# The tail of a five-part layer: products over two scan tiles at once, residual sums on TensorE, token moves spread over eight rounds

## The reference, cut to what matters

```
# branch 1: two Mamba scans, forward and over the flipped sequence (256 inner channels, 16 states)
h = exp(dt_t[..., None] * A) * h + (dt_t * u_t)[..., None] * B_t[:, None, :]
y_t = einsum('bdn,bn->bd', h, C_t)
...
y = (y + u * D) * silu(z);  out = einsum('bld,ed->ble', y, Wout)
# branch 2: attention over 16 heads, then one of 8 experts for each token
x = x + (o @ wo + bo)
hn2 = layernorm(x) * ln2_g + ln2_b
idx = argmax(hn2 @ gate_w + gate_b, axis=-1)
mid = relu(einsum('th,ehf->etf', hn2, w1) + b1[:, None, :])
y = einsum('etf,efh->eth', mid, w2) + b2[:, None, :]
moe = y[idx, arange(T)];  out = x + moe
# the layer
x = x + branch1(xn) + branch2(xn)
```

## Time and profile before

| | us |
|---|---|
| runs | 1390.32, 1390.54, 1390.70 |
| median | 1390.54 |
| profiled execution, its own time | 1392.7 |
| its span, first to last instruction | 1391.0 |
| begin of the tail stage | 874.5 |
| first scan tile to end of the last | 877.1 to 1379.0 |

### The profile page before, as it was taken

One profiled execution on the slowest core, in us unless ns is written; L12 is line 12 of the kernel. 1 busy time (PEld: TensorE's weight loads), 2 busy tenths in 40 slices (PEclk: granted clock), 3 DMA queues, 4 the chain that ended last, 5 costly groups with the idle time before them and its releaser, 6 DMA issues. The chain is left out here.

```text
span 1391.0 us, 18267 instructions
## 1 busy us (share of the span) xinstructions
PE 969.8 (70%) x5897; PEld 314.5 (23%) x5897; DVE 1212.5 (87%) x1837; ACT 871.9 (63%) x1298; POOL 520.8 (37%) x484
## 2 busy tenths in 40 slices
PE   3789986888888888888888888434326775743243
PEld 1443321111111111111111111212103443411011
DVE  8872668999999999999999980799989997978997
ACT  6445557777777777777777789444346665644332
POOL 4030116000000000000000000669899997979985
PEclk9999997999999999999999999655557988865555
DMA  3033333100000320000011000144578778785540
GB/s 96 0 139 132 125 125 141 49 1 1 1 28 27 62 58 13 20 28 17 16 32 28 6 14 2 44 89 108 133 183 181 179 182 203 182 204 122 122 103 8
DMA packets 88865, 111.49 MB, mean 80 GB/s; under 512 B 15603, under 2 KB 46122, under 8 KB 88770
## 3 DMA queue, kind: packets, MB, share of 16 engines
q1 hardware_dynamic: 87746, 108.22, 29.9%
q0 software_dynamic: 1024, 2.10, 0.6%
HBM read 84.43 MB, written 25.56 MB: 79 GB/s over the span
## 5 line engine op out<-in xcount | busy, mean ns | idle before, releaser
L829 DVE TENSOR_REDUCE at_mpart<-psum 128x1 f32<-128x512 f32 x1024 | 637.9, 684 | 44.4 <-PE psum L977 41.0
L805 ACT ACTIVATE at_probs<-psum 128x1024 f32<-128x1024 f32 x512 | 495.2, 1021 | 147.5 <-PE psum L1005 147.2
L1328 POOL TENSOR_TENSOR t_inject<-shared 128x512 f32<-128x512 f32 x256 | 326.1, 1304 | 31.3 <-DMA shared<-mp_dtu_d 18.6
L1018 PE MATMUL psum<-at_probs,at_vg 128*32 128x512 f32 x2048 | 274.8, 609 | 0.5 <-ACT at_probs L805 0.4
L977 PE MATMUL psum<-at_ks,at_qs 56*128 56x512 bf16 x1024 | 203.3, 394 | 100.4 <-DVE at_mpart L829 99.6
L1687 PE MATMUL psum<-t_hc,stack 128*32 128x512 f32 x512 | 108.1, 929 | 190.6 <-DVE t_hc L1502 180.9
L698 POOL CAST at_m<-at_mneg 128x16 bf16<-128x16 f32 x16 | 3.1, 196 | 579.8 <-DVE at_mneg L834 572.8
L1380 ACT ACTIVATE psum<-shared,aneg 128x512 f32<-128x512 f32 x256 | 175.9, 692 | 58.8 <-DVE t_hc L1502 34.7
L1576 DVE TENSOR_TENSOR_SCAN psum<-psum,t_last,t_inject 128x512 f32<-128x512 f32 x142 | 179.7, 1281 | 13.6 <-issue 11.1
L1005 PE MATMUL psum<-at_qs,at_ks 59*128 59x512 bf16 x1024 | 158.0, 380 | 7.3 <-ACT at_probs L805 5.8
L977 PEld LDWEIGHTS psum<-at_ks,at_qs 56*128 56x128 bf16 x1024 | 49.4, 93 | 424.7 <-DVE at_mpart L829 410.2
(11 more groups left out here) (221 smaller groups left out, 895.4 us busy)
## 6 DMA issues: line engine op xcount, KB each, us to landing
shared<-mp_dt_d SPq DMA_DIRECT2D x64, 256.0 KB, 5.5
shared<-mp_dtu_d SPq DMA_DIRECT2D x64, 256.0 KB, 9.1
shared<-mp_bc_d SPq DMA_DIRECT2D x256, 64.0 KB, 2.1
t_w<-in_w SPq DMA_DIRECT2D x46, 256.0 KB
mp_u_d<-shared SPq DMA_DIRECT2D x8, 512.0 KB, 4.5
mp_z_d<-shared SPq DMA_DIRECT2D x8, 512.0 KB, 4.6
mp_dt_d<-shared SPq DMA_DIRECT2D x8, 512.0 KB, 2.8
mp_dtu_d<-shared SPq DMA_DIRECT2D x8, 512.0 KB, 2.7
```

The source lines that it names most:

```text
L805: act.activation(probs[:, u_ % 2, p, :], s_pair[p], ACT.Exp, scale=float(HD) ** -0.5).then_inc(probs_ready, 1)
L829: dve.reduce_max(mpart[:, s % 2, 2 * jp + b, i, kc:kc + 1], ring[x % 3], AX.X).then_inc(ring_free, 1)
L1018: mm = pe.matmul(o_bank[VW * j:VW * (j + 1), :], vg[:, g % 2, kt, j, :], probs[:, u_ % 2, j // 2, CH * (j % 2):CH * (j % 2 + 1)], start=(k ...
L1328: pool.tensor_tensor(inject[:, k % NI, :], dus[:, i % 2, j, :], bs[:, m % NBC, :], ALU.mult).then_inc(injected, 1)
```

## The change

- **Wide products.** POOL forms the inject of two tiles in one instruction of 1024 columns (at even k; B's row is broadcast over both), which waits until both slots are free. DVE multiplies tiles 1 and 2 of a round by C in one instruction after tile 3 has been scanned; tile 0 (where POOL doesn't have it) and tile 3 (unless POOL has it) stay single. `groups` and `ends_at` hold this; `on_pool` gives POOL tile 0 of each round and tile 3 of each third (before: tile 2 of each fourth), none in the rounds of the moves: 64 tiles instead of 70.
- **Sums on TensorE.** `attended_out` and two of the four `experts_out` are gone; `project_out` instead starts its PSUM sum with an identity product over 512 columns of xn1 (n = 0 to 3) or of the gathered rows (n = 6 and 7).
- **Standardize on ACT.** 16 activations (k = 14 to 17) with scale and shift replace the 16 DVE instructions; DVE forms the shift (k = 11). They write to `x`, so that xn1 stays as it was until the gather.
- **Token moves.** One indirect DMA after each two tiles: scatter in rounds 11 to 18, gather in rounds 55 to 62 (chunks 1, 2, 3, 0).
- **Experts.** Choice at k = 28 to 32 and numbering at k = 36 to 38; the slots take three rounds of each four, 20 to 50. ACT's three side steps stand at other tiles of the round; `chunk_out` one tile pair later; POOL's constants (`numbering`) after the second inject.

```diff
-        GATHER = 49
-        SCATTER = 13
+        GATHER = 55
+        SCATTER = 11
+        MOVE = 8
...
-            return not SCATTER <= r < SCATTER + 4 and not GATHER <= r < GATHER + 4 and (j == 0 or j == 2 and r % 4 == 1)
+            return not SCATTER <= r < SCATTER + MOVE and not GATHER <= r < GATHER + MOVE and (j == 0 or j == 3 and r % 3 == 1)
+        def groups(r):
+            tiles_ = [j for j in range(NJ) if not on_pool(NJ * r + j)]
+            return {4: [(0, 0), (1, 2), (3, 3)], 3: [(1, 2), (3, 3)], 2: [(1, 2)]}[len(tiles_)]
...
         def slot_at(r, shift):
-            s = r - FIRST_SLOT - shift
-            return s if 0 <= s < NSLOT else None
+            n, rest = divmod(r - shift - FIRST_SLOT, 4)
+            s = 3 * n + rest
+            return s if rest < 3 and 0 <= s < NSLOT else None
...
-                if k >= NI:
-                    pool.wait_ge(scanned, k - NI + 1)
-                pool.tensor_tensor(inject[:, k % NI, :], dus[:, i % 2, j, :], bs[:, m % NBC, :], ALU.mult).then_inc(injected, 1)
+                if k % 2 == 0:
+                    if k >= NI:
+                        pool.wait_ge(scanned, k - NI + 2)
+                    pool.tensor_tensor(inject[:, k % NI:k % NI + 2, :], dus[:, i % 2, j:j + 2, :],
+                                       bs[:, m % NBC, :].unsqueeze(1).to_broadcast([P, 2, CH]), ALU.mult).then_inc(injected, 2)
                 weigh(k - NI + 1)
-                if SCATTER * NJ <= k < SCATTER * NJ + NT:
-                    scatter(k - SCATTER * NJ)
+                if k % 2:
+                    if SCATTER <= r < SCATTER + MOVE:
+                        scatter((k - SCATTER * NJ) // 2)
+                    if GATHER <= r < GATHER + MOVE:
+                        gather((k - GATHER * NJ) // 2)
...
+            def standardize(c):
+                act.wait_ge(shift_ready, 1)
+                for i in range(TPC * c, TPC * (c + 1)):
+                    act.activation(xn[:, i, :], S.xn1[:, i, :], ACT.Identity, bias=shift[:, i:i + 1], scale=rstd[:, i:i + 1])\
+                        .then_inc(xn_ready, 1)
...
                     else:
-                        act.wait_ge(dve_weighed, by_dve[k - ND] + 1)
+                        act.wait_ge(dve_weighed, part_of[k - ND])
...
                 if m == 0:
+                    if (s := slot_at(r - 3, -1)) is not None:
+                        turned(s)
+                if m == 2:
                     if (s := slot_at(r - 2, 1)) is not None:
                         result(s)
-                if m == 1:
+                if m == 3:
                     if (s := slot_at(r - 2, 0)) is not None:
                         hidden(s)
...
-                dve.tensor_tensor(hc[:, r % 2, j, :], decay[k % ND], cs[:, m % NBC, :], ALU.mult).then_inc(dve_weighed, 1)
+                dve.tensor_tensor(hc[:, r % 2, j:j + n, :], decays[:, j:j + n, :],
+                                  cs[:, m % NBC, :].unsqueeze(1).to_broadcast([P, n, CH]), ALU.mult).then_inc(dve_weighed, 1)
...
-                if 9 <= k < 9 + NCH:
-                    attended_out(k - 9)
-                    standardize(k - 9)
+                if k == 11:
+                    shifts()
...
-                    if GATHER + 5 <= r < GATHER + 5 + NCH:
-                        experts_out(r - GATHER - 5)
+                    if r in (GATHER + 5, GATHER + 7):
+                        experts_out(2 + (r - GATHER - 5) // 2)
...
             def project_out(n):
                 out = take("O", n)
+                c = n if n < NCH else NN - 1 - n
+                more = S.xn1 if n < NCH else moved if c < 2 else None
+                if more is moved and n >= NCH:
+                    pe.wait_ge(gathered[c], 16 * TPC)
+                if more is not None:
+                    pe.matmul(out, S.ident[:, :], more[:, TPC * c:TPC * (c + 1), :].rearrange("p i d -> p (i d)"),
+                              start=True, stop=False)
                 pe.wait_ge(y_free, NB * (n + 1))
```

More of the change, by code:

```diff
@@ L1171, in tail_stage @@
         oT = y[:, 0:NT, :].rearrange("p i d -> p (i d)")
-        xn = moved = S.xn1
+        xn, moved = x[:, 0:NT, :], S.xn1
         x_dram, y_dram = (nc.dram_tensor(f"t_{n}", [NSLOT * P, P], F32).ap() for n in ("rows", "done"))
+        decays = S.psum[:, 0:ND * CH].rearrange("p (j t) -> p j t", t=CH)
         decay, y_bank, ring = S.banks[0:ND], S.banks[ND], S.banks[ND + 1:8]
@@ L1281, in _, with numbering @@
         def _(pool):
[L1282 to L1291, removed]
+            def numbering():
+                pool.memset(zeros[:, :], 0.0).then_inc(zeros_ready, 1)
+                pool.iota(rank_i[:, :], pattern=[[-1, NE]], base=NE, channel_multiplier=0).then_inc(pool_c, 1)
+                pool.iota(step_i[:, :], pattern=[[P, NT]], base=0, channel_multiplier=0).then_inc(pool_c, 1)
+                pool.iota(slot_i[:, :], pattern=[[1, NSLOT]], base=0, channel_multiplier=0).then_inc(pool_c, 1)
+                pool.memset(every[:, :], 1.0).then_inc(pool_c, 1)
+                pool.memset(first[:, :, :], 1.0).then_inc(pool_c, 1)
+                pool.wait_ge(pool_c, 5)
+                pool.memset(first[:, :, 0:1], 0.0).then_inc(pool_c, 1)
+                pool.affine_select(out=before[:, :], in_=every[:, :], compare_op=ALU.is_gt, fill=0.0, base=0,
+                                   pattern=[[1, P]], channel_multiplier=-1).then_inc(pool_c, 1)
             def scatter(i):
@@ L1405, in _ @@
                 if m == 0:
+                    if (s := slot_at(r - 3, -1)) is not None:
+                        turned(s)
+                if m == 2:
                     if (s := slot_at(r - 2, 1)) is not None:
                         result(s)
-                if m == 1:
+                if m == 3:
                     if (s := slot_at(r - 2, 0)) is not None:
                         hidden(s)
-                if m == 2:
-                    if (s := slot_at(r - 2, -1)) is not None:
-                        turned(s)
-                if m == 3 and 5 <= r < 7:
-                    normed(2 * r - 10)
-                    normed(2 * r - 9)
+                if k in (21, 24):
+                    normed(0 if k == 21 else 2)
+                    normed(1 if k == 21 else 3)
+                if 14 <= k < 14 + NCH:
+                    standardize(k - 14)
                 if k == 10:
@@ L1491, in weigh @@
             def weigh(k):
-                if k < 0 or on_pool(k):
+                if k not in ends_at:
                     return
-                i, q, j = at(k)
-                r = k // NJ
+                k0 = ends_at[k][0]
+                i, q, j = at(k0)
+                r, n = k0 // NJ, k - k0 + 1
                 m = NQ * (i // NB) + q
@@ L1520, in chunk_out, with shifts @@
                 res_free.append((emptied["dve"], EMPTIED[USE["O", n]][1]))
-            def standardize(c):
+            def shifts():
                 dve.wait_ge(rstd_ready, 1)
-                dve.wait_ge(res_c, c + 1)
-                for i in range(TPC * c, TPC * (c + 1)):
-                    dve.tensor_scalar(xn[:, i, :], S.xn1[:, i, :], mv[:, i, 0:1], rstd[:, i:i + 1],
-                                      ALU.subtract, ALU.mult).then_inc(xn_ready, 1)
-            def attended_out(c):
-                add_to(S.res[:, TPC * c:TPC * (c + 1), :], S.xn1[:, TPC * c:TPC * (c + 1), :]).then_inc(res_c, 1)
-                res_free.append((res_c, c + 1))
+                dve.scalar_tensor_tensor(shift[:, :], mv[:, :, 0], -1.0, rstd[:, :], ALU.mult, ALU.mult).then_inc(shift_ready, 1)
             def experts_out(c):
@@ L1667, in project_out @@
                         mm = pe.matmul(out[:, P * i:P * (i + 1)], gated[:, n % 2, b, P * i:P * (i + 1)], S.w_out[:, n // NCH, b, :],
-                                       start=(b == 0), stop=(b == NB - 1))
+                                       start=(b == 0 and more is None),
+                                       stop=(b == NB - 1 and (more is None or i == TPC - 1)))
                 mm.then_inc(side_full, 1)
```

72 lines of the change are left out of this document (41 added, 31 removed).

## The result

The changed kernel takes 1354.9 us (1352.3 to 1357.7) where the kernel before takes 1390.4: ratio 0.9746, interval 0.972 to 0.9772. The forecast was 1362.5 with a range of 1348 to 1384; the time lies inside, 7.6 us under the likeliest value. The profiled execution took 1357.19 of its own (span 1355.5), against 1364.7 in the sum.

The account below looks back on a forecast made before the run. DVE and POOL were both taken to set the pace, with DVE also stalled behind late dt*u. Gains of -41.5 us and added waits of +13.5 gave -28.0, from 1390.5 to 1362.5 us, range 1348 to 1384.

Parts of the forecast that it names:

- The stalls: DVE's waits behind late dt*u tiles: with slots spread, SP's issues keep up, so -15.5 of 16.7 us.
- Rival 1: The dt*u stalls stay despite the spread slots, since DMA queues remain nearly full: +15.5, 1378 us; chance 0.12.
- The moves: Scatter and gather rounds: POOL no longer paces them, DVE's 11.1 us of waits shrink to about 3, -8 us.
- The sums: Adds to res go to PE, standardize steps to ACT, less the new shift: -15.0 us of DVE's work in all.
- the waits at the start: At the start DVE waits for the next decay, +2 us, and logits are read closer behind PE, +1.
- The weigh's "0": DVE's wide weigh: pairs at 1.11 to 1.12 us save what six more tiles on DVE take back, 0.
- 128 W - 307: POOL's excess over DVE in us, for a start-to-start price W of a wide inject; 2.31 assumed.
- Rivals 2 and 3: POOL's wide inject costs 2.57 us (kernel 1377, chance 0.10) or the median 2.80 (kernel 1407, chance 0.07).
- +3.5 for `turned`: Decay banks of tiles 1 and 2 come free only with the wide weigh; decays 0.4 us late in nine rounds.
- +3 for POOL: In rounds with two products and two wide injects POOL needs 7.2 us against DVE's 5.8: +3 us.
- The end: Before the last projection PE's identity product runs while DVE gates, with a wait on each side: +1 us.
- The lock: DVE instructions with two SBUF inputs wait while POOL works, each behind a longer POOL instruction: +3 us, bounds 0 and +8.

Follow-up runs that it names:

- e9: Changed kernel with the 23 stores of expert results issued by ACT instead of SP: 1347.7 us, ratio 0.9686.
- e13: Changed kernel with two more small DMA issues per expert on SP, copies of the b1 load that nobody reads: 1373.2 us, ratio 0.9858.
- e1: Changed kernel with its expert slots one per round again (24 rounds) instead of three in four rounds: 1369.9 us, ratio 0.9843.
- e3: Changed kernel with scatter and gather over four rounds each, one row move per scan tile, instead of eight rounds: 1369.0 us, ratio 0.9844.
- e4: Changed kernel with the four adds of xn1 and the 16 standardize steps back on DVE: 1361.4 us, ratio 0.9788.
- e5: Changed kernel with every weigh product of DVE one tile wide, POOL's inject still wide: 1355.4 us, ratio 0.9744.
- e11: Changed kernel with both POOL's inject and DVE's weigh one tile wide again: 1352.5 us, ratio 0.972.
- e2: Changed kernel with POOL's inject one tile at a time, DVE's weighs still wide: 1355.4 us, ratio 0.9738.

## Where the prediction was right, and where not

**The stalls: cause right, SP's level too low.** SP's list was the cause (e9, e13; e1 takes away issues and bytes at once). The step that failed is its count: "In eight rounds: ... = 56.6 us" and "With six experts in eight rounds it is 50.3 against 51.7: just enough". The rows give 62.9 and 56.7. The difference, 6.2, is what was foreseen (6.3); the level was 6.3 too low at both ends, since the B and C rows behind dt*u were counted at 3.63 instead of 6.5 and the experts at 3.16 each, where six took some 23 with the weight issues that were held up and the gaps ahead of them. So SP still needs 4 us more than DVE (52.8, two blocks of 26.4) in such eight rounds, and 8.1 us of waits stayed where 1 was foreseen. Rival 1 (all stay) fell; about half of its waits are there. That the spread was nevertheless worth 13.9 to 17.1, near the term's 15.5, is luck: without it the changed kernel would wait 24.5 us (e1) and not the 16.7 of the kernel before.

**The moves: right in kind, too small.** -8 was foreseen from waits of 11.1; undoing it costs 13.4. The term was read off the kernel before, and there the eight rounds with moves weren't all paced by POOL: the scatter's took 7.1, 7.1, 8.5 and 9.9 us, the gather's 8.4 and three times 9.8, 70.3 in all. In e3 all eight run at POOL's pace, 77.8. So in the kernel before POOL's lead covered some of the moves, and in e3 hardly any. A reason that fits is that a wide inject waits for two free slots of four, so that POOL leads by two pairs and not by four tiles; no run shows it (four-round moves with narrow injects would).

**The sums: right.** -11.1 for them and +3 for the waits at the start make -8; e4 gives 6.3. DVE's busy time came to 446 of 449 foreseen.

**The width.** The weigh's "0" holds (pairs take 1.12 to 1.14 start to start; e5, e11). The inject cost 2.37 to 2.40, not 2.31. What failed is the formula "128 W - 307": at e2's 2 x 1.26 to 1.29 it gives 15 to 23 us, and the stretch shows 2.7. It took every us of POOL above DVE's bare work as lost, but POOL has 32 us of waiting for DVE to spare (23.4, 4.8 and 4.4), 22 of them before 970, where DVE normalises, waits for ACT, chooses and numbers. The weigh's width has a price too, the 4.4 us of DVE's work in e5, which the waits for dt*u hide. Rivals 2 and 3 were thus priced too high: a pair at 2.57 would have cost some 3 us, not 15, and I gave them 0.17 of the chance.

**The added waits.** +3.5 for `turned` and +3 for POOL came to the 3.0 us before t_hp, one piece of 0.2 and five of 0.5 to 0.8, at tile 0 of rounds 24, 27, 39, 48 and 51, not in rounds of index 1 modulo 3. The profile names no releaser, but its rows show it: each of these scans starts 0.09 us after a wide inject has ended, while its decay had been there for 1.8 to 2.8 us. So these are POOL's, as much as the 3 foreseen though in other rounds, and the 3.5 for `turned` came to nothing. The end cost 0.9 of the 1 foreseen.

**The lock.** +3 was foreseen, about 0 came. Some waits did get longer (t_rank 2.35, one wide inject, where e2 has 0.29), but they are fewer: t_full fell from 1.29 to 0.28, and in e2 it is back at 1.29. In the changed kernel six such instructions of over 0.6 us take 11.5 us in all, in e2 nine take 12.5. The Trainium skill (SBUF - State Buffer, "Who interferes with whom") calls it an exclusive lock; t_rank agrees. I had priced the length and not the number of meetings. Nor is the length bounded by one instruction of POOL. In e11, with narrow products, an instruction of 128 columns took 3.38, where the next one of its kind takes 0.29, while POOL ran one product behind the other, of 1.3 us each:

```profile
940.51 3.38 DVE L1481 TENSOR_TENSOR t_pick<-t_lg,t_top 128x128 f32<-128x128 f32 x1
```

```profile
939.96 1.34 POOL L1347 TENSOR_TENSOR t_inject<-shared 128x512 f32<-128x512 f32 x1
941.20 1.32 POOL L1334 TENSOR_TENSOR t_hc<-t_hp,shared 128x512 f32<-128x512 f32 x1
942.43 1.31 POOL L1347 TENSOR_TENSOR t_inject<-shared 128x512 f32<-128x512 f32 x1
```

It ended 0.15 us after the last of the three. The add of 4.28 us in the earlier trace rows likewise outlasts a run of four narrow injects, from 1310.30 to 1315.23. So "one narrow inject longer than now" was the wrong measure: what counts is how long POOL goes on without a pause.

By single runs: slots 13.9, moves 13.4, early sums 6.3, width 0 to 3: 34 to 36 of the 37.1 us of stretch. Parts that hang together needn't add up (the spread alone gave 17.1, taken out it cost 13.9), and the two adds of gathered rows that went to PE, half of the earlier trace rows's 7.9, weren't run alone. The forecast's errors had both signs: the stalls kept 7 us more than foreseen, while the moves brought 5 more, the added waits cost 3.5 less and the lock 3 less. That the sum missed by only 7.6 is in part luck.

## What to carry to other kernels

A queue that issues DMAs is an engine with a budget: take its interval between two late transfers from the trace, over more than one stretch, not a sum of single issues, and compare it with what the compute engines need. If it is longer, move issues to an engine that has time, as here 23 stores to ScalarE (6 us). Where two engines are near balance, price a slower one by its waits for the other first: 13 us more work on POOL cost under 3.

## What the runs showed that was not expected

- 23 stores issued by ACT, 0.33 us each (7.6 us, DVE's waits for decays 5.8 as before), freed 2.4 us in eight rounds on SP and gave 6. The Trainium skill (DMA: Bandwidth & Descriptors, "Issuing engines are not separate DMA queues") says that initiating DMAs on several engines saves only the sequencer's time, "usually small relative to the DMA itself". The first half agrees; here that time was the bound.
- An issue's price depends on what was issued ahead: eight of 64 KB take 3.63 us, and 6.50 right behind 1 MB of dt*u.
- A product's width moved the kernel's time by nothing that can be told, though 1024 columns cost POOL 2.39 against 2.52 to 2.58 for two of 512, and the narrow weighs cost DVE 4.4 us of work. Both prices went into waits that were there anyway.
- A DVE instruction with two SBUF inputs can wait through several of POOL's instructions, where they follow each other without a pause: 3.38 us beside narrow products (e11), 2.35 beside one wide one.
